# Copies of segment marks in 16-row pieces, and the norm of two blocks moved to the next stage

## The reference

```
x = layernorm(x + L0(x))   # 10 hops: h = 0.9 * norm * segment_sum((h * norm)[src], dst) + 0.1 * x
x = layernorm(x + L1(x))   # 2 GAT layers, 4 heads of 64, then a linear map
x = layernorm(x + L2(x))   # relational convolution, 8 edge types
x = layernorm(x + L3(x))   # graph attention with 8 heads and a feed-forward part
```

## Time and profile before

| | us |
|---|---|
| median of 3 runs (3374.46 to 3377.92) | 3375.05 |
| the profiled execution, its own time | 3375.13 |
| its span in the trace | 3373.5 |
| PE busy in the span | 2122.9 |
| DVE busy | 2171.8 |
| POOL busy | 1821.5 |
| ACT busy | 1245.3 |

### The profile page before, as it was taken

One profiled execution on the slowest core, in us unless ns is written; L12 is line 12 of the kernel. 1 busy time (PEld: TensorE's weight loads), 2 busy tenths in 40 slices (PEclk: granted clock), 3 DMA queues, 4 the chain that ended last, 5 costly groups with the idle time before them and its releaser, 6 DMA issues.

```text
span 3373.5 us, 42846 instructions
## 1 busy us (share of the span) xinstructions
PE 2122.9 (63%) x14275; PEld 1837.1 (54%) x14276; DVE 2171.8 (64%) x5824; ACT 1245.3 (37%) x1339; POOL 1821.5 (54%) x1791
## 2 busy tenths in 40 slices
PE   2875999999999255666546666652333343555455
PEld 1554999999998244444434444432333333554444
DVE  7997777767768177666747888873433335555555
ACT  1986667666765223333233333320000002222222
POOL 3333222222221377777477777727777776777771
PEclk7987999999999577777767777776666666666667
DMA  2100000000000444444255555422222223444441
GB/s 63 24 1 1 0 0 0 0 0 0 0 0 15 149 129 140 139 139 135 78 153 154 145 145 148 138 88 53 59 59 58 59 61 117 132 132 132 133 123 38
DMA packets 133665, 264.99 MB, mean 79 GB/s; under 512 B 33930, under 2 KB 77558, under 8 KB 133446
## 3 DMA queue, kind: packets, MB, share of 16 engines
q0 software_dynamic: 72208, 188.45, 20.6%
q1 hardware_dynamic: 24614, 50.78, 4.7%
q10 hardware_dynamic: 36692, 23.93, 2.2%
HBM read 235.41 MB, written 27.85 MB: 78 GB/s over the span
## 4 chain that ended last, share of the span: by engine, by line
POOL 32%; DVE 13%; issue 12%; PE 8%; DMA 2%; ACT 1%; ACTq 1%; POOLq 0%; DVEq 0%
POOL t_rows L2190 12%; POOL t_rows L2611 11%; POOL t_rows L2945 9%; DVE t_rows L2390 3%; PE t_sum_ps L2298 2%; DVE t_own L1978 2%; DVE t_onehot L2117 1%; PE t_product_ps L1924 1%; ACTq L1821 1%; PE t_sum_ps L3005 1%; PE t_sum_ps L2632 1%; DMA t_rows<-kv_table_b,t_src 0%; PE t_small_ps L2984 0%; DVE t_stage L3029 0%; DVE t_so_far L2361 0%
## 5 line engine op out<-in xcount | busy, mean ns | idle before, releaser
L2190 POOL DMA_INDIRECT t_rows<-gat_table,t_src x806 | 770.9, 956 | 354.1 <-issue 242.5
L1238 PE MATMUL hop_ps<-parts,wide 128*128 128x256 f32 x5900 | 713.8, 284 | 4.0 <-DVE parts L1334 2.8
L1238 PEld LDWEIGHTS hop_ps<-parts,wide 128*128 128x128 f32 x5900 | 711.2, 192 | 6.0 <-issue 3.5
L1289 ACT CAST wide<-counts 128x3200 fp32r<-128x3200 fp8e4 x177 | 506.2, 2863 | 230.9 <-PE hop_ps L1238 211.3
L2298 PE MATMUL t_sum_ps<-t_rows,t_onehot 128*128 128x264 f32 x1660 | 468.9, 451 | 101.7 <-DVE t_rows L2390 101.7
L2611 POOL DMA_INDIRECT t_rows<-rel_table_b,t_rel x403 | 385.0, 955 | 181.0 <-issue 180.1
L1299 POOL CAST wide<-counts 128x3200 fp32r<-128x3200 fp8e4 x59 | 168.7, 2859 | 580.7 <-PE hop_ps L1238 564.6
L2298 PEld LDWEIGHTS t_sum_ps<-t_rows,t_onehot 128*128 128x128 f32 x1660 | 372.1, 228 | 182.3 <-issue 104.8
L2945 POOL DMA_INDIRECT t_rows<-kv_table_b,t_src x403 | 384.1, 953 | 137.1 <-issue 120.9
L2632 PE MATMUL t_sum_ps<-t_rows,t_onehot 128*128 128x128 f32 x830 | 147.2, 360 | 295.1 <-DMA t_rows<-rel_table_b,t_rel 295.1
L2632 PEld LDWEIGHTS t_sum_ps<-t_rows,t_onehot 128*128 128x128 f32 x830 | 143.0, 272 | 303.9 <-issue 301.3
(11 more groups left out here) (452 smaller groups left out, 3332.0 us busy)
## 6 DMA issues: line engine op xcount, KB each, us to landing
t_dst_wide<-dst_row SPq DMA_DIRECT2D x72, 544.0 KB, 4.1
t_rows<-gat_table,t_src POOLq DMA_INDIRECT x806, 2.9
rel_table_b<-t_stage ACTq DMA_DIRECT2D x25, 512.0 KB, 3.3
t_rows<-rel_table_b,t_rel POOLq DMA_INDIRECT x403, 2.5
t_rows<-kv_table_b,t_src POOLq DMA_INDIRECT x403, 2.8
gat_table<-t_own ACTq DMA_DIRECT2D x10, 520.0 KB, 5.2
kv_table_b<-t_fresh ACTq DMA_DIRECT2D x5, 512.0 KB, 2.9
out<-x SPq DMA_DIRECT2D x6, 256.0 KB
```

Of the source, the lines that this page charges most:

```text
L1238: last = nc.tensor.matmul(ps[bank][0:columns.shape[-1], 0:2 * D], columns[:, k, :], parts[old][:, k, :], start=(k == 0), stop=(k == NB - 1))
L1289: nc.scalar.copy(wide[b % B][:, :, :], column(b)).then_inc(widened, 1)
L2190: c.nc.gpsimd.indirect_dma_start(t.rows[:, slot(k), 0:FW], None, self.table, bass.IndirectOffsetOnAxis(ap=t.src[:, k:k + 1], axis=0)).then ...
```

## The change

Two things are done. First, the four DMAs of line 1696 copy only rows 0 to 15 of the marks, and one more DMA copies row 16 to the four partitions of that position, with a source that is repeated four times. The semaphore count that DVE waits for goes from 4 to 5 DMAs. Second, the norm of the set of blocks 20 and 21 is no longer done in the last hop. It is done on DVE in the table stage, ahead of that of the last set, and PE waits for it ahead of turning that set.

```diff
@@ propagate_dense, last hop
-                    if b in SET_DONE and b < NB - 1:
+                    if b in SET_DONE and SET_DONE[b] < len(SETS) - LATE_NORMS:
                         then(norm_set(c, then, norm_tiles, SETS[SET_DONE[b]], lambda n: c.x[:, n, :]))
+LATE_NORMS = 2
...
+SPRAYED = CAP // 16 * 16
+SPREAD = HEADS + CAP - SPRAYED
@@ Enter.sp
         for h in range(HEADS):
-            sp.dma_start(t.fresh[h:HEADS * CAP:HEADS, :, :], c.cut_windows).then_inc(self.spread, 16)
+            sp.dma_start(t.fresh[h:HEADS * SPRAYED:HEADS, :, :], c.cut_windows[0:SPRAYED, :, :]).then_inc(self.spread, 16)
+        for k in range(SPRAYED, CAP):
+            sp.dma_start(t.fresh[HEADS * k:HEADS * (k + 1), :, :], c.cut_windows[k:k + 1, :, :].to_broadcast([HEADS, NB, SPAN + 1])).then_inc(self.spread, 16)
@@ Enter.pe, turn(i)
-            if i == len(SETS) - 1:
-                pe.wait_ge(self.last_normed, 1)
+            if i >= len(SETS) - LATE_NORMS:
+                pe.wait_ge(self.last_normed, i + 1 - (len(SETS) - LATE_NORMS))
@@ Enter.dve
-        norm_set(c, then, t.norm, SETS[-1], lambda b: c.x[:, b, :]).then_inc(self.last_normed, 1)
-        dve.wait_ge(self.last_normed, 1)
+        for i in range(LATE_NORMS):
+            norm_set(c, then, t.norm, SETS[i - LATE_NORMS], lambda b: c.x[:, b, :]).then_inc(self.last_normed, 1)
+            dve.wait_ge(self.last_normed, i + 1)
@@ layers_by_blocks
-                dve.wait_ge(enter.spread, 16 * HEADS)
+                dve.wait_ge(enter.spread, 16 * SPREAD)
```

## The result

The changed kernel takes 3344.3 us (median of 4 runs, 3342.8 to 3345.92) against 3376.34 for the kernel before beside it. The ratio is 0.9907, with a 95% interval of 0.9894 to 0.9920. The profiled execution has a span of 3342.1 us against 3373.5. The forecast was 3345.

What follows compares the result with a forecast made beforehand. One DMA engine, carrying the 17-row copies of the marks, was taken to stall ACT's stores in the table stage. Terms 3.49 + 22.91 + 1.2 + 2.46 = 30.1 us off 3375.1 gave 3345.0, range 3342 to 3351 for 8 in 10.

Steps and rivals of the forecast that it cites:

- The cause: Table stage: a 17-row copy goes to one DMA engine of 16, seen as share 0.07; the marks take 31 us.
- The norm in the hop: End of last hop: without the norm of blocks 20 and 21, DVE and the barrier end 3.49 us earlier.
- The norm in the table stage: The added norm on DVE costs 0, with 7 us of cover before PE; some 8 us of slack left.
- The two stalls and the last set: Table stage: two ACT store issues fall to 0.38 us each, minus 22.91; last set takes 2.8 us for 3.98.
- The landing: The table's last store lands in 4.4 us instead of 6.86, bounds 3.4 to 6.9.
- The copies of the marks: Table stage: four rows per engine load it 1.8 to 3.4 us before the first stores, none on the path.
- Rival 1: DMA engines become the table stage's bound, traffic ending at 1110.1: 3347.7 to 3351 us, chance 0.12.
- Rival 2: Copies of the marks are not spread, stalls stay, only the hop's gain remains: 3371.6 or 3369.8 us, chance 0.03.
- Rival 3: Marks limited at their source to 28 GB/s in all, delaying stores on every engine: 3382.8 us, chance 0.02.
- The 30 us: The first gather starts 30.0 us earlier, and the shift goes through the layers to the program's end.

Runs made afterwards that it cites:

- whole heads: Changed kernel with one or two heads' marks copied as 17 rows: 3352.64 and 3360.4 us; 0 is the changed kernel, 4 the kernel before.
- the copies alone: Changed kernel with the norm of blocks 20 and 21 back in the last hop, marks still split: 3347.2 us, ratio 0.9921.
- the second execution: The changed kernel run again unaltered, beside other runs on the same chip: 3346.19 us, ratio 0.9907 of the kernel before.

## Why the prediction was right

- **The cause.** One DMA engine held the stage. The share of 0.07 was read as 1 of 16, and the runs with 0, 1, 2 and 4 whole heads confirm it: each head adds 6.6 to 7.2 us. The packet records do too, with never more than one row of marks in flight before, for 36.0 us; the forecast had 31, without the stores in between. The forecast and the kernel differ by 0.7 us. So close a hit is luck: the terms below miss by 1 to 2 us with both signs, and the changed kernel's second median was 3346.19.
- **The norm in the hop**, minus 3.49: measured 3.40.
- **The norm in the table stage**, cost 0 on DVE: it ends at 1089.23 and PE turns the blocks at 1098.14, with 9 us of cover. DVE's wait for products is still 9.2 us, where I had said 8. What the step missed is what else hangs on an earlier begin: the stage runs longer at half clock and is 1.2 to 1.4 us longer than with the copies alone. The clock's part of that is in the last store (0.5 to 1.65 us); the rest lies in its landing.
- **The two stalls and the last set**, minus 24.1: the last store was issued at +41.95 and is at +19.19 and +18.03, minus 22.8 and 23.9. The two differ as their stretches at half clock do, which end 8.0 and 5.5 us into the stage.
- **The landing**, 4.4: measured 2.64, and some 3.6 in the second execution of the same kernel. In the profiled execution the landing's error (1.8 us better) and the last store's (1.3 us worse) nearly cancel.
- **The copies of the marks**, 1.8 to 3.4 us of load for an engine: a row took 0.82 us on average in the packet records, so four rows 3.3 (0.76 and 3.0 in the second execution). The upper bound was the better one.
- **Rival 1**, the transfers as the bound, holds in part: the share is 0.99 in the stage's second half, and 1.0 to 1.2 us go when the marks are moved out. It did not reach the 1110.1 that I gave it. Rival 2 (no spreading, 0.07 again) is refuted by the rows of marks, 16 at once instead of one, and by the missing stalls. Rival 3 (marks limited at their source, 28 GB/s in all) is refuted by their time: 0.87 MB in the 4.9 us from 1088.8 to 1093.7, some 177 GB/s.
- **The 30 us reached the end.** The part behind the first gather took 2234.90 against 2235.24.

## What to carry to other kernels

A window in which every compute engine idles and the DMA share is near 1/16 meant here that one DMA engine had all the work. Look at the outer size of the copies issued just before: four copies of 17 rows moved their rows one after another in 36 us, the same rows as 16 and one apart took 5. A long issue on an engine is a symptom, and it stood here on another queue than the copy that caused it. The same fault was worth nothing where nobody waited for the queue behind it, so follow the chain first.

## What the runs showed of the hardware that I had not expected

- The half clock came at the seam in every run, but not at a fixed place. In the twelve profiled executions with 2.19 to 7.09 us of idle time on PE at the seam, a stretch at 0.50 began 2.1 to 4.9 us behind the end of the tail product, in some of them when PE was already at work on the stage. Two executions of the same kernel differ in it by 2.4 us. With 20 or 10 more products and 1.30 or 1.00 us of idle time left, the clock stayed at 1.00.
- 17-row copies issued by POOL are spread (up to 9 rows in flight at once, stage 23.07), those issued by SP are not (never more than one, stage 49.58).
- A 12,850-byte row took 0.49 us when one engine copied the marks alone, and 0.82 and 0.76 in two executions in which all did.
